# Two cross-attention layers on one core: fixed order tables per batch, with tables of their own for the first and last batch, and layer 0's row bias formed by the vector engine

## The reference

```
x:   [8, 512, 256]    ctx: [8, 1601, 128]     all float32
layer 0: q = x Wq + bq;  k = ctx Wk + bk;  v = ctx Wv + bv
         w = softmax(q k^T / 16, over the 512 rows of x)      (axis=1)
         y = layernorm(w v + x) * gamma + beta
layer 1: q = y Wq + bq;  k = ctx Wk + bk;  v = ctx Wv + bv
         out = y + (softmax(q k^T / 16, over the 1601 rows of ctx) v) Wo + bo
```

## Time and profile before

| | us |
|---|---|
| three runs, median | 513.74 (513.39 to 514.05) |
| profiled execution, its own time | 513.53 |
| its span, first to last instruction | 511.7 |
| PE busy | 464.3 (91%) |
| DVE busy | 387.2 (76%) |
| ACT busy | 385.2 (75%) |
| POOL busy | 346.2 (68%) |

### The profile page before, as it was taken

How to read it: one execution, slowest core, us unless ns; L and a number is a source line. 1 busy time by engine, 2 the same in 40 slices (tenths; PEclk the granted TensorE clock), 3 DMA queues, 4 the chain that set the end, 5 groups by cost and what they waited for, 6 DMA issues and landing times.

```text
span 511.7 us, 7981 instructions
## 1 busy us (share of the span) xinstructions
PE 464.3 (91%) x2426; PEld 381.0 (74%) x2426; DVE 387.2 (76%) x920; ACT 385.2 (75%) x798; POOL 346.2 (68%) x319
## 2 busy tenths in 40 slices
PE   8659887999989998999899998999899998799776
PEld 8447555888778886888688885888688886587675
DVE  2355579769986899769977898679976998669744
ACT  3576956998689967997789966987799867872452
POOL 0195966896787948896688857896689768971400
PEclk9989978999999999999999999999999999999989
DMA  8400030000040005000140005000220001000101
GB/s 241 114 0 1 1 106 0 2 2 0 7 141 2 1 1 146 3 0 1 33 115 1 1 2 147 1 0 1 66 83 0 2 3 41 0 1 10 34 0 42
DMA packets 23897, 17.31 MB, mean 34 GB/s; under 512 B 1055, under 2 KB 23854, under 8 KB 23854
## 3 DMA queue, kind: packets, MB, share of 16 engines
q1 hardware_dynamic: 23850, 16.79, 11.4%
q10 hardware_dynamic: 4, 0.00, 0.0%
HBM read 12.59 MB, written 4.19 MB: 33 GB/s over the span
## 4 chain that ended last, share of the span: by engine, by line
PE 41%; DVE 36%; ACT 8%; issue 8%; DMA 4%; POOL 2%; SPq 0%; DVEq 0%; POOLq 0%; ACTq 0%
DVE p1T_lo L884 7%; PE ps_s L432 5%; DVE xr L938 5%; PE ps_l L432 5%; PE ps_l L433 5%; PE ps_s L434 5%; PE ps_l L434 5%; PE ps_s L433 5%; DMA x_sb<-in_x_dram 4%; DVE xr L899 4%; PE ps_s L546 4%; DVE s_sb L872 3%; DVE max L951 3%; DVE y_res L978 2%; DVE xhat L930 2%
## 5 line engine op out<-in xcount | busy, mean ns | idle before, releaser
L1069 POOL TENSOR_TENSOR p_lo<-p,p_hi 128x512 fp32r<-128x512 f32 (+1 forms) x104 | 135.2, 1307 | 83.4 <-ACT p_hi L750 83.4
L1062 POOL TENSOR_TENSOR wsum<-wsum,p 128x512 f32<-128x512 f32 (+1 forms) x88 | 115.0, 1307 | 4.6 <-ACT p L742 1.3
L736 ACT ACTIVATE p<-s_sb,min 128x512 f32<-128x512 f32 (+1 forms) x104 | 75.3, 725 | 18.8 <-DVE min L872 16.8
L884 DVE TENSOR_TENSOR p1T_lo<-ps_s,p1T_hi 128x512 fp32r<-128x512 f32 (+1 forms) x104 | 68.0, 681 | 26.7 <-ACT p1T_hi L787 26.5
L787 ACT CAST p1T_hi<-ps_s 128x512 fp32r<-128x512 f32 (+1 forms) x104 | 59.1, 585 | 30.7 <-PE ps_s L546 18.1
L872 DVE CUSTOM_DVE_ANT_0 s_sb<-ps_l,cb 128x512 f32<-128x512 f32 (+1 forms) x104 | 69.8, 683 | 12.5 <-PE ps_l L434 8.9
L742 ACT ACTIVATE p<-p,r 128x512 f32<-128x512 f32 (+1 forms) x104 | 73.1, 719 | 4.4 <-DVE r L879 3.9
L951 DVE TENSOR_REDUCE max<-ps_s 128x1 f32<-128x804 f32 x60 | 59.1, 994 | 15.7 <-PE ps_s L434 13.3
L750 ACT CAST p_hi<-p 128x512 fp32r<-128x512 f32 (+1 forms) x104 | 63.4, 618 | 1.3 <-PE ps_l L434 0.7
L546 PE MATMUL ps_s<-ident,p 128*128 128x128 f32 (+1 forms) x416 | 58.7, 279 | 5.0 <-ACT p L779 5.0
L546 PEld LDWEIGHTS ps_s<-ident,p 128*128 128x128 f32 (+1 forms) x416 | 50.4, 145 | 14.6 <-ACT p L779 7.3
(11 more groups left out here) (163 smaller groups left out, 1063.8 us busy)
## 6 DMA issues: line engine op xcount, KB each, us to landing
ctx_sb<-in_ctx_dram SPq DMA_DIRECT2D x24, 256.0 KB, 4.9
x_sb<-in_x_dram SPq DMA_DIRECT2D x8, 512.0 KB, 4.2
out_dram<-y_res SPq DMA_DIRECT2D x16, 256.0 KB, 2.2
p<-in_L_xattn_Wq_dram SPq DMA_DIRECT2D x2, 256.0 KB, 3.7
ctx_sb<-in_ctx_dram SPq DMA_DIRECT2D x8, 32.5 KB
p<-in_L_xattn_Wk_dram SPq DMA_DIRECT2D x2, 128.0 KB, 3.8
p<-in_L_xattn_Wv_dram SPq DMA_DIRECT2D x2, 128.0 KB, 4.3
p<-in_L_xattn_Wo_dram SPq DMA_DIRECT2D x1, 256.0 KB, 4.7
```

What stands on the lines that cost most here:

```text
L736: nc.scalar.activation(p0[0:m, ring0(i), :], s0_sb[0:m, (a.par + i) % 2, :], ACT.Exp, bias=min0[0:m, i:i + 1], scale=-1.0, accum_out=sum0[ ...
L884: nc.vector.tensor_tensor(p1T_lo[0:m, i % RING, :], ps_turn[i % 3][0:m, :], p1T_hi[0:m, i % RING, :].bitcast(F32), ALU.subtract).then_inc( ...
L1062: nc.gpsimd.tensor_tensor(total, total, p0[0:m, ring0(i), :], ALU.add).then_inc(wsum_done, 1)
L1069: nc.gpsimd.tensor_tensor(p0_lo[0:m, h, :], p0[0:m, ring0(i), :], p0_hi[0:m, h, :].bitcast(F32), ALU.subtract).then_inc(p0_lo_done, 1)
```

## The change

There are six parts.

1. Orders. The body tables go. Each step has a place, a number, in one of three tables for each engine (`STEADY`, `FIRST` for batch 0, `LAST` for batch 7); batch n is set off by 100,000 a batch, and the steps of all batches are sorted by place (`program`). A batch spans three slots, as before. The making of layer 1's weights (`pre1`) becomes the steps `prepare` 0 to 3 (PE), 0 to 4 (ACT) and 0 to 5 (DVE) with places in batch 0. `bias_row1`, `bias_x0`, `normalised` and POOL's `gamma_y` and `beta_y` (together `residual1` before) are now placed one by one for each of four row tiles.
2. Row bias. The six matmuls of `project_bias0` go. DVE forms u0 . x for each row of x by four `x_bias` (a product and a sum over 256 elements, written into a column), and PE turns each column, broadcast to 128 x 128, into `ps_misc`. `bias0` (ACT) copies it as before. u0 is made as a row by two matmuls in place of four.
3. Batch 0's `weigh0` is one float32 matmul on `p0` itself instead of three on its parts, and has no `p0_high` and no `p0_low` (`IN_FLOAT`).
4. Buffers. `p0` is a ring of five across the batches, and `exp0` waits for `p0_low` and `sum_weights` of the tile five back, no longer for `weigh0`.
5. The last batch's layer 1 lies wholly in `ps_l0`, its exponentials in the buffers of x, ctx and p0; each of its score blocks waits for the exponentials of the block just before.
6. SP issues the loads of batch n + 2 and then the store of batch n, in one loop.

```diff
+def program(places, batches):
+
+
+    steps = []
+    for n in range(batches):
+        own = {**places[STEADY], **(places[FIRST] if n == 0 else places[LAST] if n == batches - 1 else {})}
+        steps += [(SLOT * n + at, n, name, i) for (name, i), at in own.items() if at is not None]
+    return [(n, name, i) for _, n, name, i in sorted(steps)]
...
+    LAST: {
+        ("turn_x", 0): 11253, ("turn_x", 1): 14955, ("project_q0", 0): 18821, ("project_bias0", 0): 28845,
...
-        def s1_banks(b, t):
-
-
-            return (ps_l0 if last(b) and t % 2 else ps_s1)[:].rearrange("p (k m) -> p k m", m=BANK)
...
+        def s1_banks(b):
+            return (ps_l0 if last(b) else ps_s1)[:].rearrange("p (k m) -> p k m", m=BANK)
...
             def project_bias0(a, _):
-                for c in range(EC):
-                    mm = split3(ps_misc[:], u0_hi[:, c, :], u0_lo[:, c, :], xT_hi[:, c, :], xT_lo[:, c, :],
-                                start=(c == 0), stop=(c == EC - 1))
+
+                pe.wait_ge(x_bias_done, TB * (a.n + 1))
+                for t in range(TB):
+                    mm = nc.tensor.transpose(ps_misc[:, t * P:(t + 1) * P], x_bias_col[:, t:t + 1].broadcast_to([P, P]),
+                                             ident[:])
                 mm.then_inc(cb_ps, 1)
...
+                if a.n in IN_FLOAT:
+                    pe.wait_ge(norm0_done, MT * a.n + i + 1)
+                    mm = nc.tensor.matmul(ps_acc0[:], ctx_sb[a.par][0:m, i, :], p0[0:m, ring0(a, i), :], **ends)
...
-                before = t - 2 if last(b) else t - 1
-                if before >= 0 and k in (0, len(chunks) - 1):
-
-                    pe.wait_ge(exp1_done, 2 * (TB * b.n + before) + (1 if k == 0 else 2))
+                if t == 0 and k in (1, 2) and not first(b) and not last(b):
+                    pe.wait_ge(o_done, 2 * (b.n - 1) + k)
+                if t and k in (0, len(chunks) - 1):
+                    pe.wait_ge(exp1_done, 2 * (TB * b.n + t - 1) + (1 if k == 0 else 2))
...
-            def pre1():
-                turn_weights(1, s1_bank(0), s1_bank(1))
-                pe.wait_ge(wv_loaded, 16 * 3)
...
+            def prepare(_, i):
+
+                if i == 0:
+                    turn_weights(1, s1_bank(0), s1_bank(1))
+                    pe.wait_ge(wv_loaded, 16 * 3)
...
             def exp0(a, i):
                 act.wait_ge(s0_read, MT * a.n + i + 1)
-                if (held := before0(a, i)) is not None:
-                    back, last = held
-                    act.wait_ge(pv0_ps, MT * (a.n - back) + last + 1)
-                    act.wait_ge(wsum_done, summed(a.n - back, last))
+                k = MT * a.n + i - R0
+                if k >= 0:
+                    act.wait_ge(wsum_done, k + 1)
+                if k >= 0 and k // MT in split:
+                    act.wait_ge(p0_lo_done, halves(batch(k // MT), k % MT) + 1)
+                elif k >= 0:
+                    act.wait_ge(pv0_ps, k + 1)
...
+            def x_bias(a, t):
+                if t == 0:
+                    dve.wait_ge(made_sb, 2)
+                    dve.wait_ge(x_loaded[a.par], 16 * (a.use + 1))
+                if t == 0 and not first(a):
+                    dve.wait_ge(cb_ps, a.n)
+                if t >= 2:
+                    dve.wait_ge(x_bias_done, TB * a.n + t - 1)
+                nc.vector.tensor_tensor_reduce(out=x_u0[:, t % 2, :], in0=x_sb[a.par][:, t, :], in1=u0_row[:], scale=1.0, scalar=0.0,
+                                               op0=ALU.mult, op1=ALU.add, accum_out=x_bias_col[:, t:t + 1]
+                                               ).then_inc(x_bias_done, 1)
```

More of the change, by code:

```diff
@@ L684, in _ @@
             steps = {f.__name__: f for f in (
[L685 to L695 removed]
+                turn_x, project_q0, project_bias0, turn_ctx, scores0, weigh0, sum_rows0, predict, turn_y, project_q1, scores1,
+                turn_p1, weigh1, project_out, prepare)}
+            pre0()
+            held = None
+            for n, name, i in after_start(TENSOR):
+                if name in MISC:
+                    if held:
+                        misc_read(*held)
+                    held = name, batch(n), i
+                steps[name](batch(n), i)
         @blk.scalar
@@ L706, in ctx_split @@
                 act.wait_ge(ctx_loaded[a.par][g], 16 * (a.use + 1))
[L707 removed]
+                if a.n >= 2:
                     act.wait_ge(pv1_ps, MT * (a.n - 2) + group(g)[-1] + 1)
@@ L838, in _ @@
+            steps = {f.__name__: f for f in (
+                x_turned, q0_high, bias0, ctx_high, ctx_split, exp0, norm0, p0_high, weighed0, y_turned, q1_high, exp1,
+                p1_turned, weighed1, prepare)}
+            pre0()
+            for n, name, i in after_start(SCALAR):
+                steps[name](batch(n), i)
         @blk.vector
@@ L1044, in _ @@
+            steps = {f.__name__: f for f in (
+                ctxT_low, xT_low, at0_low, x_bias, bias_x0, q0_low, max0, recip0, residual0, moments0, normalised, bias_row1, q1_low,
+                rowmax1, bias1_of, recip1, p1_low, finish, prepare)}
+            pre0()
+            for n, name, i in after_start(VECTOR):
+                steps[name](batch(n), i)
         @blk.gpsimd
```

603 lines of the change are left out of this document (325 added, 278 removed), and 211 rows, old and new, of tables (GPSIMD, GPSIMD_ORDER, SCALAR, SCALAR_ORDER).

## The result

The changed kernel is slower by 0.7%. 14 runs of each gave a median of 519.43 us (517.09 to 523.26) for it and 516.17 us (513.39 to 519.01) for the kernel before; the ratio is 1.007 [1.0038, 1.0101], 3.6 us more, where 11 us less were forecast.

What follows compares the result with a forecast made beforehand. PE was taken to set the pace in the middle, with waits at both ends. Terms -6.3 - 3.6 - 8.0 + 7.0 = -10.9 gave a forecast of 502.5 us, range 489 to 514.

Steps and rivals of the forecast that it cites:

- Term A: Row bias: project_bias0 goes from six matmuls to four turns, saving PE 1.06 us a batch over six batches, -6.3 us.
- Term B: Middle batches: PE's waits for q1_low and the load of x shrink, partly given back for x_bias on DVE; -3.6 us.
- The forecast's own sign: Middle: forecast is wrong if a batch takes under 54 or over 56 us.
- Rival 3: Middle: DVE takes over the pace through x_bias at 5.7 us a batch; +11, 525 us; chance 0.12.
- Term C: Start, to batch 0's turn_y: later project_q0, but spread preparation and less work on ACT and POOL; -8.0 us.
- rival 1: Middle and start run clean: B -10.2, C -11, D +5; sum -22.5, 491 us; chance 0.22.
- Term D: Last batch: earlier turn_y -3.2, score blocks serial on one bank set +8.7, half clock +1.5; +7.0 us.
- number 2: Ends give the gain back: start only -3, last batch +12.5 at half clock; -0.4, 513 us; chance 0.13.

Runs made afterwards that it cites:

- the two runs with 16 turns: project_bias0 turns each column four times, 16 turns in place of 4: on the changed kernel 530.21 us, on it with GpSimd pause and two bank sets 503.36 us.
- the pause: Changed kernel, with GpSimd waiting after a batch's second rsqrt_var until all four normalised are through (batch 1 left as it was); 0.9751, 504.30 us.
- The kernel with all repairs: Changed kernel with GpSimd paused in every batch, two sets of banks for the last batch's score blocks, and prepare 0 behind project_q0; 0.9459, 489.20 us.
- the kernel before with only the pause: Kernel before, with GpSimd waiting after a batch's second rsqrt_var until the four bias_row1 are through; 0.9570, 495.42 us.

## Why the prediction was wrong

**Term A, -6.3: right.** 32 turns (L650), forecast at 0.35 us for four; the two runs with 16 turns put it at 7.6 us over eight batches, 0.95 each, to within some 3 us in all.

**Term B, -3.6: this is the step that failed.** The wait for `q1_low` did go, and that for x nearly. The `x_bias` were sized at 1.2 us each and took 0.42 in the median, 0.50 in the mean; `bias_row1` fell from 1.17 to 0.68 in the mean. What failed is a cost that stood nowhere in the sum. I looked for GpSimd's contention only at the instructions that were new, and left `normalised` at its old 0.41, at a place where the new order of GpSimd had put four instructions beside it. Its mean went from 0.44 to 1.07. From first to last `turn_y` the stretch is 391.9 us with the stall and 376.3 without: 15.6 us. Without it the middle would have come out as forecast: from `turn_y` of batch 0 to the last `weigh1` of batch 6, a mark that the change did not move, it is 378.4 us (both at their start), before 389.5, so 11.1 us less over seven batches, where 1.66 a batch, 11.6, were forecast. With the stall it is 393.9. The forecast's own sign came as well: 285.0 / 5 = 57.0 us a batch, over its limit of 56. The order of GpSimd's steps was there to be read, rows 6 had the stall on `bias_row1`, and the trace of before even had it on `normalised`: the 1361 ns above are the fourth one of batch 0, beside a `p0_low`, again through 0.15 us behind it. What was missing was to lay the one order over the other for each vector instruction on PE's path. Rival 3 named the contention, but as VectorE's load and through `x_bias`. That was not the main loss: VectorE is busy 48.6 us a batch (242.98 / 5), not 52.3, and with `x_bias` taken off, PE's wait for `xhat` stayed at 19.7 us and the time within 5 us.

**Term C, -8.0: nearly right, in part by errors that cancel.** `turn_y` of batch 0 came 6.9 us earlier (71.3). `project_q0` started at 17.52, forecast 17.4, and batch 0's last `weigh0` was through at 58.3, forecast 58. From there to `turn_y` it took 13.0 us, where 10.7 were forecast, because the stall stood here too (four `normalised` in 3.68 us); with the pause it took 10.1. Against that stand the 1.4 us that I had given back for two `weigh0` of batch 1. With the pause `turn_y` came at 67.0, 11.2 us earlier than before, the end that I gave to rival 1, but not all of it is the pause's: the last `weigh0` was through 1.4 us earlier there (56.9), which a pause behind it can't bring, and the granted clock from `project_q0` to it was 0.96, in the changed kernel 0.89. What float32 matmuls in batch 0 (part 3) bring or cost was not tried by itself.

**Term D, +7.0: mis-sized, +9.4.** Its parts: from the last `weigh1` to the first score 3.3 us in place of 7.1, -3.8 (forecast -3.2); four blocks 25.6 in place of 13.8, +11.8 (forecast +8.7, and +1.5 for the clock; the distances at full clock were exactly 5.5, and the two blocks that began at half clock cost 3.0 us more, not 1.5); the rest of the end +1.3. That rest I had put at nothing. The 16 turns took the same 3.3 us at half clock in both kernels, but behind them the six `weigh1` took 2.7 us in place of 1.5: before, the full clock was back at the second of them, here only at the last. The run with two sets of banks gives the change of banks 13.3 us by the ratio. The earlier start, -3.8, was real, but the own order of the last batch costs 2.8 us one batch earlier, as the run without it shows.

**The sum.** -6.9 (start), +4.5 (middle, forecast -9.9 over six batches), +9.4 (end) = +7.0 in the traces, +3.6 in the ratio. Of the rivals, number 2 had the end and number 3 the right resource; my error was to see them as alternatives, at 0.13 and 0.12. Their causes are independent of one another, and together they need neither of their extremes. A stall of 15.5 us and the end's +9.4 make 24.9; against them stand the middle without the stall, -11.1, and the start, -6.9, and +6.9 is left. The range, up to 514, did not hold the two side by side.

**Open.** The kernel with all repairs takes 54.7 us a batch in the middle (273.3 / 5), the kernel before with only the pause 54.0, although PE has 1.06 us less to do in the first. Of these 0.7 us the own order of the last batch is 0.6: without it the same five batches take 270.2, 54.0 each. What stays open is why it is not some 53. No wait of PE in that stretch is over 0.7 us a batch, and no run tells which of them it is.

## What to carry to other kernels

When an order changes on one engine, lay the engines' orders over each other and ask for every instruction on the critical path what GpSimd does at that moment; a vector instruction that reads and writes SBUF is not of fixed length (`normalised` took 0.40 to 1.50 us). Where GpSimd has slack, one semaphore wait that keeps it still during a short critical stretch of VectorE may be worth more than all reordering: here 22 us for one line. And a wait of PE in each batch does not make PE's work free: 1.06 us of it a batch came back as some 0.95 beside such a wait, as it would where what PE waits for hangs on PE's own earlier work.
